# A GRU and a four-way selective scan on one core: one C product in twelve moved from VectorE to GpSimd, and the logarithm taken with its rounding remainder

## The reference, cut to what matters

```python
x_dbl = einsum('bkdl,kcd->bkcl', xs, x_proj_w)            # K = 4 directions, 192 channels
dts, Bs, Cs = split(x_dbl, [R, R + N], axis=2)            # N = 16 states
dts = softplus(einsum('bkrl,kdr->bkdl', dts, dt_projs_w) + dt_projs_b[...])
As  = -exp(A_logs).reshape(K, DI, N)
def step(h, inp):                                         # over the 196 tokens
    u_t, d_t, B_t, C_t = inp
    h = h * exp(d_t[..., None] * As) + (d_t * u_t)[..., None] * B_t[:, :, None, :]
    y = einsum('bkcn,bkn->bkc', h, C_t)
    return h, y
...
y = y_0 + flip(y_2) + transpose(y_1) + transpose(flip(y_3))   # then norm, gate, out_proj, residual
```

## Time and profile before

| what | value |
|---|---|
| median of 3 runs (lowest to highest) | 3240.07 us (3240.0 to 3241.2) |
| the profiled execution | 3240.27 us |
| its span | 3238.3 us |
| granted TensorE clock, mean | 0.991 |
| scan stage: first scan starts, last readout starts | 1022.8 us, 3203.0 us |
| busy over the span: PE, DVE, ACT, POOL | 86%, 83%, 56%, 69% |

### The profile page before, as it was taken

The page is one execution under the profiler, slowest core; times in us unless marked ns, Lnnn a source line. Parts: engine busy times, 40 slices in busy tenths (PEclk is TensorE's granted clock), DMA queues, the critical chain, the costliest instruction groups (busy, mean ns, idle before and its releaser), DMA issues.

```text
span 3238.3 us, 101526 instructions
## 1 busy us (share of the span) xinstructions
PE 2779.2 (86%) x39496; PEld 2070.2 (64%) x39496; DVE 2672.7 (83%) x4226; ACT 1824.2 (56%) x3872; POOL 2243.0 (69%) x1878
## 2 busy tenths in 40 slices
PE   4999999999996788888888888888888888888886
PEld 4999999986664555555555555565555655656554
DVE  6444444445776999999999999999999999999995
ACT  1111111112224677777777777777777777777773
POOL 5333333320005989989899898888989898898983
PEclk9999999999997999999999999999999999999999
DMA  5000000002334555545545555455454554555541
GB/s 199 0 0 0 0 0 0 0 5 97 112 112 140 156 156 153 153 156 149 177 140 163 159 144 169 141 160 174 134 170 149 157 163 140 162 161 155 162 146 46
DMA packets 57085, 385.29 MB, mean 119 GB/s; under 512 B 10100, under 2 KB 15060, under 8 KB 31700
## 3 DMA queue, kind: packets, MB, share of 16 engines
q1 hardware_dynamic: 57044, 384.79, 38.8%
HBM read 352.64 MB, written 32.11 MB: 119 GB/s over the span
## 4 chain that ended last, share of the span: by engine, by line
DVE 30%; PE 25%; issue 23%; POOL 16%; ACT 3%; DMA 1%; DVEq 1%; POOLq 0%; SPq 0%; ACTq 0%
DVE arena L776 15%; PE ps L1112 10%; PE ps L1121 9%; POOL arena L495 9%; DVE arena L779 9%; PE ps L1108 2%; DVE arena L793 1%; DVE conv_out L203 1%; POOL arena L471 1%; POOL arena L464 1%; POOL arena L468 1%; DVEq L773 1%; DMA x_in<-x_pair 1%; POOL arena L477 1%; POOL arena L482 1%
## 5 line engine op out<-in xcount | busy, mean ns | idle before, releaser
L1244 PE MATMUL ps<-arena,ident 128*128 128x392 f32 (+1 forms) x4096 | 1163.0, 417 | 0.9 <-DVE arena L788 0.9
L963 ACT ACTIVATE ps<-arena,abias,a 128x390 f32<-128x390 f32 x1024 | 690.0, 677 | 317.4 <-DVE arena L779 179.8
L788 DVE TENSOR_TENSOR arena<-arena,ps 128x784 f32<-128x784 f32 x768 | 745.7, 971 | 38.2 <-PE ps L1234 12.8
L1244 PEld LDWEIGHTS ps<-arena,ident 128*128 128x128 f32 x4096 | 682.8, 191 | 143.9 <-DVE arena L788 1.2
L776 DVE TENSOR_TENSOR_SCAN arena<-ps,arena 128x392 f32<-128x392 f32 x768 | 702.6, 956 | 7.4 <-POOL arena L495 6.3
L779 DVE TENSOR_TENSOR_SCAN arena<-ps,arena 128x392 f32<-128x392 f32 x768 | 702.6, 956 | 0.0
L1234 PE MATMUL ps<-arena,sel 96*128 96x196 bf16 x3072 | 391.6, 250 | 355.7 <-DVE arena L788 355.7
L1234 PEld LDWEIGHTS ps<-arena,sel 96*128 96x128 bf16 x3072 | 227.5, 97 | 665.0 <-DVE arena L788 630.7
L967 ACT ACTIVATE ps<-arena,abias,a 128x195 f32<-128x195 f32 x1024 | 477.7, 505 | 254.2 <-DVE arena L776 139.8
L495 POOL TENSOR_TENSOR arena<-arena 128x784 f32<-128x784 f32 x256 | 472.7, 1851 | 102.6 <-PE ps L1244 97.3
L495 POOL TENSOR_TENSOR arena<-arena,wx_sb 128x784 f32<-128x784 f32 x256 | 465.4, 1850 | 14.4 <-POOL arena L482 13.7
(11 more groups left out here) (175 smaller groups left out, 3295.4 us busy)
## 6 DMA issues: line engine op xcount, KB each, us to landing
wx_sb<-b_by_state SPq DMA_DIRECT2D x64, 1568.0 KB, 6.3
wh_sb<-b_by_state SPq DMA_DIRECT2D x64, 1568.0 KB, 6.3
arena<-b_by_image SPq DMA_DIRECT2D x128, 784.0 KB, 9.1
arena<-x_seq SPq DMA_DIRECT2D x4, 2352.0 KB, 15.9
x_in<-x_pair SPq DMA_DIRECT2D x16, 588.0 KB, 4.2
x_dram<-x SPq DMA_DIRECT2D x16, 588.0 KB, 2.8
x<-x_dram SPq DMA_DIRECT2D x16, 588.0 KB, 10.0
out<-xhat SPq DMA_DIRECT2D x16, 588.0 KB, 2.8
```

Of the source, the lines that this page charges most:

```text
L788: dve.tensor_tensor(h, h, bank(3), ALU.mult).then_inc(s["readout_ready"], 1)
L963: ins = act.activation(r, src, ACT.Exp, scale=a01[:, c:c + 1], bias=abias01[:, c:c + 1])
L1244: mm = pe.matmul(ps[:, 5 if g < 8 else 6, 0:cols], ident[:, :], h[:, m * cols:(m + 1) * cols], start=(opens and m == 0), stop=(closes and ...
```

## The change

1. **Group 3's product with C goes from VectorE to GpSimd** in each phase (`pool_read`). GpSimd cannot take C from PSUM, so TensorE no longer spreads it for this group; SyncE writes the two states' C of both images to DRAM (two small DMAs) and broadcasts them to all partitions (`c_chunk`, 401 KB). GpSimd multiplies after drive 6.
2. **Group 3's sum comes two groups later**, after that of group 5 (`BEHIND`), and the ring's waits follow this order: drive 9, which takes group 3's buffer, waits for it.
3. **The logarithm.** The polynomial and `choose` go. ScalarE now forms 1 + e, takes 1 off it again, and takes the logarithm; GpSimd adds back what the addition rounded off, e - ((1 + e) - 1). GpSimd has four steps in place of five, two after drive 10 and two after drive 11; VectorE has none; ScalarE keeps four operations.

```diff
+POOL_READS = (3,)
+DVE_READS = GRP - len(POOL_READS)
+READ_LEAD = 3
+BEHIND = 2
-SMALL = 0.022
...
+        def dve_reads_before(g):
+            return g - sum(r < g for r in POOL_READS)
+        def reduce_order():
+            order, late = [], []
+            for g in range(GRP):
+                if g in POOL_READS:
+                    late.append(g)
+                else:
+                    order.append(g)
+                order += [r for r in late if r + BEHIND == g]
+            return order
+        ORDER = reduce_order()
...
+                for q, g in enumerate(POOL_READS):
+                    for img in range(2):
+                        sp.dma_start(c_by_state[k][q, :, img, :], xdbl[N * img + 2 * g:N * img + 2 * g + 2, T:T2]
+                                     ).then_inc(s["c_spilled"], 16)
...
+            def spread_c(P, k, first=False):
+                sp.wait_ge(s["c_spilled"], (P + 1) * (32 * len(POOL_READS)))
+                if not first:
+                    sp.wait_ge(s["pool_read"], P * len(POOL_READS))
+                rows = c_by_state[k].rearrange("q n i t -> (q n i t)").unsqueeze(0)
+                sp.dma_start(c_chunk[:, :], rows.broadcast_to([128, len(POOL_READS) * GC])).then_inc(s["c_chunk_in"], 16)
...
                         next_x(i)
+                    if ahead and max(POOL_READS) + READ_LEAD < 8:
+                        spread_c(P1, k1)
                     if ahead:
                         spread_b(P1, k1, 1)
...
                 if n == 0:
                     pool.wait_ge(s["soft_step"], P * 4 + 3)
-                    pool.tensor_tensor(poly, poly, soft, ALU.mult).then_inc(s["series_step"], 1)
+                    pool.tensor_tensor(rest, soft, rest, ALU.subtract).then_inc(s["rest_ready"], 1)
                 elif n == 1:
                     pool.wait_ge(s["soft_step"], P * 4 + 4)
-                    pool.wait_ge(s["series_step"], P * 2 + 1)
-                    pool.tensor_tensor(poly, poly, lnp, ALU.subtract).then_inc(s["series_step"], 1)
+                    pool.wait_ge(s["rest_ready"], P + 1)
+                    pool.tensor_tensor(lnp, lnp, rest, ALU.add).then_inc(s["log_ready"], 1)
                 elif n == 2:
-                    pool.wait_ge(s["series_step"], P * 2 + 2)
-                    pool.tensor_tensor(lnp, lnp, relu, ALU.add).then_inc(s["log_ready"], 1)
-                elif n == 3:
-                    pool.wait_ge(s["choice_ready"], P + 1)
                     pool.wait_ge(s["log_ready"], P + 1)
...
-                    pool.tensor_tensor(delta[b], lnp, poly, ALU.add).then_inc(s["delta_ready"], 1)
+                    pool.tensor_tensor(delta[b], lnp, relu, ALU.add).then_inc(s["delta_ready"], 1)
...
-                    pool.wait_ge(s["reduced"], G - (RING - 1))
+                    before = st * GRP + g - RING
+                    place = before // GRP * GRP + ORDER.index(before % GRP)
+                    pool.wait_ge(s["reduced"], G - (st * GRP + g) + (place + 1))
...
+            def pool_read(P, st, g, G):
+                _, _, view = group_aps(g)
+                h = view(hb[(st * GRP + g) % RING])
+                q = POOL_READS.index(g)
+                if q == 0:
+                    pool.wait_ge(s["c_chunk_in"], P * 16 + 16)
+                pool.wait_ge(s["scan_done"], G * 2 + 2)
+                pool.tensor_tensor(h, h, view(c_chunk[:, q * GC:(q + 1) * GC]), ALU.mult).then_inc(s["pool_read"], 1)
...
                         drive(P, st, g, i * (K4 * GRP) + (st * GRP + g), head and st * GRP + g < RING)
+                        if g - READ_LEAD in POOL_READS:
+                            pool_read(P, st, g - READ_LEAD, i * (K4 * GRP) + (st * GRP + (g - READ_LEAD)))
...
-                            for n in (0, 1, 2) if g == 10 else (3, 4):
+                            for n in (0, 1) if g == 10 else (2, 3):
...
-            def choose(P):
-                dve.wait_ge(s["series_step"], P * 2 + 2)
-                dve.scalar_tensor_tensor(poly, soft, SMALL, poly, ALU.is_lt, ALU.mult
-                    ).then_inc(s["choice_ready"], 1)
...
-                        read_out(st, g, G)
-                        if g == 8 and not (last and st == K4 - 1):
-                            choose(i * K4 + (st + 1))
+                        if g not in POOL_READS:
+                            read_out(i * K4 + st, st, g, G)
...
-                    act.activation(poly, soft, ACT.Square, scale=3.0 ** -0.5, bias=series_bias[:, 0:1]
-                        ).then_inc(s["soft_step"], 1)
+                    act.activation(lnp, soft, ACT.Copy, bias=1.0).then_inc(s["soft_step"], 1)
                 else:
                     act.wait_ge(s["soft_step"], P * 4 + 2)
-                    act.activation(poly, poly, ACT.Copy, bias=13.0 / 16.0).then_inc(s["soft_step"], 1)
-                    act.activation(lnp, soft, ACT.Ln, bias=1.0).then_inc(s["soft_step"], 1)
+                    act.activation(rest, lnp, ACT.Copy, bias=-1.0).then_inc(s["soft_step"], 1)
+                    act.wait_ge(s["soft_step"], P * 4 + 3)
+                    act.activation(lnp, lnp, ACT.Ln).then_inc(s["soft_step"], 1)
...
-                            pe.wait_ge(s["readout_ready"], G)
-                        spread(g, st)
-                        if not opening:
+                            pe.wait_ge(s["readout_ready"], P * DVE_READS + dve_reads_before(g))
+                        if g not in POOL_READS:
+                            spread(g, st)
+                        if not opening and (g - 1) % GRP not in POOL_READS:
...
                             reduce(*((st, g - 1) if g else ((st - 1) % K4, GRP - 1)))
+                        if g - 1 - BEHIND in POOL_READS:
+                            r = g - 1 - BEHIND
+                            pe.wait_ge(s["pool_read"], P * len(POOL_READS) + (POOL_READS.index(r) + 1))
+                            reduce(st, r)
```

More of the change, by code:

```diff
@@ L55, in build @@
     b_by_image = nc.dram_tensor("b_by_image", [K4, 2, N, T], F32)
+    c_by_state = nc.dram_tensor("c_by_state", [K4, len(POOL_READS), 2, 2, T], F32)
     with ExitStack() as ctx:
@@ L76, in build @@
         ident = sb("ident", [128, 128])
+        c_chunk = sb("c_chunk", [128, len(POOL_READS) * GC])
         sel = sb("sel", [96, N, 3, 128], BF16)
@@ L153, in build @@
         lnp = carve(TC)
-        poly = carve(TC)
+        rest = carve(TC)
         z_fin = carve(TC)
@@ L180, in build @@
             "xc_loaded", "xt_ready", "bc_ready", "xdbl_ready", "resid_ready", "mid_ready", "parts_ready",
-            "dt_ready", "dt_read", "soft_step", "series_step", "choice_ready", "log_ready", "delta_ready", "du_ready",
+            "dt_ready", "dt_read", "soft_step", "rest_ready", "log_ready", "delta_ready", "du_ready",
             "b_ready", "c_ready", "decay_ready", "drive_ready", "scan_done", "readout_ready", "reduced",
@@ L186, in build @@
             "oproj_ready", "o_ready", "out_stored", "fin_z", "fin_x1",
-            "b_spilled", "b_chunk0", "b_chunk1", "b_chunk2", "skipped")}
+            "b_spilled", "b_chunk0", "b_chunk1", "b_chunk2", "skipped",
+            "c_spilled", "c_chunk_in", "pool_read")}
         convs = ((pad01, conv01_out, 2 * H + 1, par01, s["conv01_step"]), (pad2, conv2_out, H, par2, s["conv2_step"]))
@@ L320, in _ @@
                 spread_b(0, 0, j, True)
+            spread_c(0, 0, True)
             spill_xc(PAIRS - 1)
@@ L349, in pair @@
                         next_x(i)
+                    if ahead and max(POOL_READS) + READ_LEAD < 8:
+                        spread_c(P1, k1)
                     if ahead:
                         spread_b(P1, k1, 1)
+                    if ahead and max(POOL_READS) + READ_LEAD >= 8:
+                        spread_c(P1, k1)
                     if st == 3 and not head:
@@ L509, in _ @@
             low_parts(0, 0)
-            for n in range(5):
+            for n in range(4):
                 delta_step(n, 0, 0, 0, True)
@@ L667, in step @@
                 dve.transpose(h_t[:, p, :], h_nat[:, :]).then_inc(s["h_ready"], 1)
-            dve.wait_ge(s["const_ready"], 2)
+            dve.wait_ge(s["const_ready"], 1)
             step(0, 0, True)
@@ L780, in scan, with read_out @@
                                            ).then_inc(s["scan_done"], 1)
-            def read_out(st, g, G):
+            def read_out(P, st, g, G):
                 _, bank, view = group_aps(g)
@@ L801, in pair @@
                             scan(st, g, hf, G)
-                        read_out(st, g, G)
-                        if g == 8 and not (last and st == K4 - 1):
-                            choose(i * K4 + (st + 1))
-            choose(0)
+                        if g not in POOL_READS:
+                            read_out(i * K4 + st, st, g, G)
             pair(0, True, False)
@@ L918, in read_bc @@
                     act.wait_ge(s["b_spilled"], P * 48)
+                    act.wait_ge(s["c_spilled"], P * (32 * len(POOL_READS)))
```

(7 more changed lines are left out.)

4 lines of the change are left out of this document (1 added, 3 removed).

## The result

| | before | after |
|---|---|---|
| median (lowest to highest), us | 3240.03 (3238.60 to 3241.20) | 3285.43 (3283.51 to 3288.02) |
| ratio after to before, 95% interval | | 1.0141 (1.0123 to 1.0158) |
| profiled execution, its span, us | 3240.27, 3238.3 | 3283.51, 3281.7 |
| granted TensorE clock, mean | 0.991 | 0.976 |
| first scan starts, us | 1022.8 | 1019.15 |

The kernel is 45 us slower. I had forecast 5 us slower, with a range that ended at 3270. Lines have moved: scans are L825 and L828, the readout is L837, a drive L533, GpSimd's product L553, a spread L1276, a sum L1287, `normed` L538, `affine` L1038, the last softplus read L977.

What follows compares the result with a forecast made beforehand. VectorE set the pace; its saving would be eaten by GpSimd's and TensorE's lists. +0.88 a pair times 14 (+12.3), first pair -5.3, last -0.2, start -1.5: +5.3 on 3240.27, 3245 us, range 3225 to 3270.

Steps and rivals of the forecast that it cites:

- The late sum: Drive 9 waits for group 3's later sum, starting at 18.93 us, not 13.08; GpSimd's 4.75 us lead goes.
- Phase 0: Readouts 4 and 7 wait for late spreads, 1.00 and 1.16 us: 34.19 against 34.09, +0.10.
- Phase 1: GpSimd's list from drive 9 (18.93 + 13.45 us) sets the next phase's start: 32.38 against 33.71, -1.33.
- Phase 2: affine waits for normed, delaying scans and readout 4 (2.68 us), out_proj costs 1.14: 35.85 against 34.32, +1.53.
- Phase 3: Readout 4 loses 1.57 us, TensorE falls behind, drive 9 starts at 21.41: 34.86 against 34.28, +0.58.
- a phase on VectorE alone is then 11 x 2.752 + 1.76: VectorE's groups keep their 2.752 us spacing, with 1.76 from group 3 to 4: 32.03 us a phase.
- The places outside the loop: First pair -5.3 us, last pair -0.2, and -1.5 before the first scan.
- The cost of nothing: GpSimd's product between drives 6 and 7, the two spills and the broadcast add no time.
- The port: Rival: each GpSimd product blocks VectorE for 1.85 us over the shared SBUF port, 118 us, 3363 us; chance 0.03.
- The slower rival: Waits between engines lengthen GpSimd's list from drive 9 to next scan, 0.5 to 1 us: 3262 to 3279; chance 0.25.
- GpSimd keeps its lead: Rival: drive 9 or its list has slack, only TensorE adds time, -3.2 us a pair, 3184 us; chance 0.12.
- VectorE alone sets the pace: Rival: TensorE too has room, phases of 32.03 us, -8.3 a pair, 3108 us; chance 0.05.

Runs made afterwards that it cites:

- e3: The change with group 3's sum one group later instead of two (BEHIND = 1), separate wait instruction kept: 3231.69 us, ratio 0.9977.
- e1: The change with c_ready counted so its wait again asks for G + 1, putting the scan wait back on the readout: 3268.85 us, ratio 1.0092.
- e5: e1 plus nine unread spreads of group 3 on TensorE in phase 2, ahead of the softplus-read wait: 3252.33 us, ratio 1.0041.
- e9: The change, its separate wait instruction kept, plus nine unread spreads on TensorE in phase 2: 3276.44 us, ratio 1.0114.

## Why the prediction was wrong

**The late sum: right.** Drive 9 waits 2.97, 2.79, 2.30 and 5.07 us for it in the four phases, and the list behind it has no gap (11.66 us, forecast 11.58). e3 shows the same from the other side. GpSimd's lead is gone: the first scan of phase 0 waits 0.74 us for drive 0, and that of phase 2 starts 1.99 us behind it, where the lead was 4.75.

**Phase 0: right.** Readouts 4 and 7 wait 1.00 and 1.01 us (forecast 1.00 and 1.16). e1 measured 34.18 us for the phase, forecast 34.19.

**Phase 1: the mechanism right, its clock of groups wrong.** Forecast 32.38; e1 measured 32.55, the change 33.01. The 0.46 between them are the five readouts ahead of group 6, 0.09 each, which push drive 9 from 18.93 to 19.36.

**Phase 2: the stalls right, the tail wrong.** `affine` waits for `normed`, and scans 3 and 4 and readout 4 wait 1.94, 0.25 and 0.47 in e1 (forecast 2.15, 0.31, 0.22). Readout 7 waits 1.59 in the change and 2.50 in e1, where I had 1.14 at full clock; e5, with TensorE busy, has 1.16.

**Phase 3: right.** Readout 4 waits 1.56 us (forecast 1.57); e1 measured 35.05, forecast 34.86.

**What failed are two terms.** First, the step "a phase on VectorE alone is then 11 x 2.752 + 1.76": the 2.752 was taken from the kernel before as a property of the instructions, though the change rewrites the very number that the readout waits for. I priced no edit of a semaphore's count. What changed is which wait stands between the second scan and the readout; it makes 140.00 - 138.76 = 1.24 us a pair (the change less e1, means of 14). Second, TensorE's times behind its new idle time in phase 2, which I took from rows at full clock although the same paragraph made TensorE wait. It makes 138.76 - 137.66 = 1.10 us a pair (e1 less e5). These shares hold for this order of mending; the other way round (change, e9, e5) the clock makes 0.66 and the wait 1.69. 0.38 is left against 137.28; 0.24 of it are the five pairs of e5 where the phase 2 is 0.7 us longer. 14 x (1.24 + 1.10 + 0.38) = 38.1 us, and the distance from 3245 to the profiled execution's 3283.5 is 38. The places outside the loop came to -7.0 together, as forecast, though not one by one: the first pair went from 135.8 to 130.8 us (-5.0, forecast -5.3), the first scan is 3.6 us earlier (forecast 1.5; it starts between 1018 and 1022 us in the changed runs), and from the last pair to the end it is 1.7 longer (forecast -0.2).

**The cost of nothing: right.** The product, 1.85 us, the two spills and the broadcast are hidden, as forecast.

**The rivals.** The port is out: scans take 957 ns beside a product as without. The slower rival ("GpSimd's list is longer than its rows") had the sign and nearly the size, 3262 to 3279, but not the cause: the list is as long as its rows. It was also put at one place, behind drive 9, while the costs sat ahead of it, on VectorE, and on TensorE in phase 2. "GpSimd keeps its lead" and "VectorE alone" are out by drive 9's wait. The range reached 25 us above the forecast for one rival; two causes that I hadn't priced made 33 of the 38 above it.
